# A decoder block on one core: the mixing of the cross-attention as a band with far sums, and work moved between VectorE, ScalarE and GpSimd

## What is computed

```python
emb = norm(x) + ctx
q, k, v = emb @ wq + bq, emb @ wk + bk, emb @ wv + bv
w   = pos_bias * (abs(t - j) < 64)              # 512 x 512, zero outside a band
ek  = exp(k - max over tokens of k)
ew  = exp(w - max over j of w)                  # shared by the batches
num = einsum('tj,bjd->btd', ew, ek * v)
den = einsum('tj,bjd->btd', ew, ek)
attn = (sigmoid(q) * num / den) @ wo + bo
a   = layernorm(attn + emb) * gamma + beta
out = layernorm(relu(a @ w1 + b1) @ w2 + b2 + a) * gamma + beta
```

## Time and profile before

| | us |
|---|---|
| median of 3 runs | 1067.69 (1066.9 to 1068.81) |
| the profiled execution | 1065.92 |
| its span | 1064.2 |

### The profile page before, as it was taken

The page is one execution under the profiler, slowest core; times in us unless marked ns, Lnnn a source line. Parts: engine busy times, 40 slices in busy tenths (PEclk is TensorE's granted clock), DMA queues, the critical chain, the costliest instruction groups (busy, mean ns, idle before and its releaser), DMA issues.

```text
span 1064.2 us, 18107 instructions
## 1 busy us (share of the span) xinstructions
PE 986.2 (93%) x5720; PEld 778.7 (73%) x5720; DVE 702.2 (66%) x1823; ACT 558.1 (52%) x1218; POOL 390.3 (37%) x408
## 2 busy tenths in 40 slices
PE   5889979999999979999999799998999999889987
PEld 3667765677676857777777588886777777668876
DVE  7668976366575677677778555565777777735553
ACT  4556741404030327777777644444777777754432
POOL 5211613113130366666666300115565656510030
PEclk9889989999999999999999899999999999989989
DMA  9000102000000000000001020000000000000010
GB/s 335 12 1 0 64 16 104 1 1 0 0 0 1 1 21 1 2 21 0 21 0 33 23 77 8 0 21 1 2 22 0 21 0 25 16 11 10 0 55 25
DMA packets 14332, 25.36 MB, mean 24 GB/s; under 512 B 848, under 2 KB 11208, under 8 KB 13512
## 3 DMA queue, kind: packets, MB, share of 16 engines
q1 hardware_dynamic: 14280, 24.72, 6.8%
HBM read 20.53 MB, written 2.10 MB: 21 GB/s over the span
## 4 chain that ended last, share of the span: by engine, by line
PE 70%; DVE 16%; issue 7%; ACT 4%; POOL 2%; DMA 0%; POOLq 0%; DVEq 0%; ACTq 0%
PE bank L1478 28%; PE bank L1670 5%; PE bank L1764 5%; PE bank L1622 5%; PE bank L1883 5%; PE bank L1791 4%; PE bank L1810 4%; PE bank L1776 4%; DVE conv L627 3%; PE bank L1743 2%; PE bank L1802 2%; PE bank L1633 1%; PE bank L1750 1%; DVE scores L933 1%; DVE hidden L1078 1%
## 5 line engine op out<-in xcount | busy, mean ns | idle before, releaser
L1339 ACT ACTIVATE probs<-scores,row_bias,q_rnorm 128x256 f32<-128x256 f32 (+1 forms) x256 | 143.7, 565 | 10.8 <-DVE row_bias L939 10.3
L933 DVE CUSTOM_DVE_ANT_0 scores<-bank,mask 128x256 f32<-128x256 f32 (+1 forms) x256 | 89.3, 385 | 21.5 <-PE bank L1764 17.6
L491 POOL TENSOR_TENSOR norms<-norms,minus_half 128x16 f32<-128x16 f32 x32 | 93.6, 2924 | 2.7
L1478 PE MATMUL bank<-wqkv_hi,x_hi 128*128 128x512 f32 x192 | 85.6, 446 | 2.6 <-DVE rot L907 1.4
L474 POOL TENSOR_TENSOR k_tok<-rot 128x512 f32<-128x512 f32 x32 | 41.2, 1287 | 100.7 <-DVE rot L907 100.7
L1478 PE MATMUL bank<-wqkv_hi,x_lo 128*128 128x512 f32 x192 | 77.2, 402 | 0.0
L1478 PE MATMUL bank<-wqkv_lo,x_hi 128*128 128x512 f32 x192 | 77.2, 402 | 0.0
L1764 PE MATMUL bank<-k_t,q_t 64*128 64x256 f32 (+1 forms) x512 | 67.3, 382 | 10.3 <-DVE row_max L933 8.8
L1078 DVE SCALAR_TENSOR_TENSOR hidden<-bank,lcols,hidden 128x512 f32<-128x512 f32 (+1 forms) x48 | 35.9, 749 | 60.2 <-PE bank L1478 52.5
L1776 PE MATMUL bank<-ident,probs 128*128 128x128 f32 x448 | 67.5, 280 | 5.2 <-ACT probs L1339 5.0
L1311 ACT ACTIVATE squares<-bank 128x512 f32<-128x512 f32 x64 | 38.3, 598 | 60.9 <-PE bank L1478 60.9
(11 more groups left out here) (236 smaller groups left out, 2624.0 us busy)
## 6 DMA issues: line engine op xcount, KB each, us to landing
w_stage<-in_wm_l_dram SPq DMA_DIRECT2D x8, 534.0 KB, 3.6
w_stage<-in_wqkv_dram SPq DMA_DIRECT2D x2, 1536.0 KB, 7.6
out_dram<-stream SPq DMA_DIRECT2D x4, 512.0 KB, 2.9
stream<-in_x_dram SPq DMA_DIRECT2D x1, 1536.0 KB, 12.9
emb<-in_ctx_dram SPq DMA_DIRECT2D x1, 1536.0 KB, 6.7
inner<-in_w_gate_dram SPq DMA_DIRECT2D x1, 1152.0 KB, 8.9
ew<-in_pos_bias_dram SPq DMA_DIRECT2D x1, 1024.0 KB, 9.8
w<-in_w_x_dram SPq DMA_DIRECT2D x1, 1024.0 KB, 12.8
```

The lines of the kernel that those rows point to most:

```text
L491: pool.tensor_tensor(norms[:, 2, :], norms[:, 1, :], minus_half[:, :], ALU.pow).then_inc(c_rn, 1)
L933: dve.tensor_tensor_reduce(scores[:, i % 2, e, 0:nk], bank[6 + e][:, (i % 2) * 2 * P:(i % 2) * 2 * P + nk], mask[:, 2 * P - nk:2 * P], 1.0 ...
L1339: act.activation(probs[:, i % 2, e, 0:nk], scores[:, i % 2, e, 0:nk], ACT.Exp, bias=row_bias[:, w % 2, h:h + 1], scale=q_rnorm[:, w, h:h + 1],
L1478: ins = pe.matmul(out, stationary, moving, start=(first and i == 0), stop=(last and i == len(terms) - 1))
```

## The change

- `mix_tokens`: each group of four products of 512 columns becomes four of 192, 320, 320 and 192 columns (`NEAR`), which cover the key tiles within reach of each range of tokens: 1024 columns instead of 2048.
- The rest comes as far sums. ACT sums each 128-column tile of ek and ekv over its tokens (`tile_sum`: a Copy with an accumulator, 16 for each block): those of block 0 in a row after `by_token(0)`, those of block b+1 in pairs after each of the eight Relu of `mlp_x(b)`. POOL adds two tile sums for each of three ranges (`far_keys`: three additions of 128x4), once all 16 of the block are there. DVE adds ew_t times the far sum to den and to num (`with_far`: three instructions of 192, 128 and 192 columns each), so that `gated_ratio` has 18 instructions instead of 6, and waits for `b_far` first.
- DVE's `embed` of block 2 stands ahead of `gated_ratio(1)`, and that of block 3 at the end of round 0, after `a_low(1)`.
- The four `tensor_scalar` of `norm_apply` into `inner` go from DVE to POOL (`norm_inner`), for all four blocks; DVE keeps the statistics.
- POOL's order: `far_keys(0)` stands between `keep_emb(0)` and `rstd_of(5)`; `far_keys(b+2)` stands in `finish(b)` ahead of the remaining `rstd_of`, `keep_emb` and `add_out(b)`.
- DVE's and POOL's loops over blocks are written out; PE's and ACT's stay loops.

```diff
+NEAR = ((0, 0, 192), (2, 192, 512), (1, 0, 320), (3, 320, 512))
+FAR = ((2, 3), (0, 3), (0, 1))
+FAR_RANGES = ((3, 0, 192), (3, 192, 320), (0, 320, 512))
...
+            def far_keys(b):
+
+                pool.wait_ge(b_sums, 16 * b + 16)
+                if b:
+                    pool.wait_ge(b_ratio, 8 * b)
+                for r, (j0, j1) in enumerate(FAR):
+                    pool.tensor_tensor(far_sums[:, :, r], tile_sums[:, :, j0], tile_sums[:, :, j1], ALU.add)\
+                        .then_inc(b_far, 1)
...
             keep_emb(0)
+            far_keys(0)
             rstd_of(NB + 1)
             keep_emb(1)
...
+            def norm_inner(b):
+
+                rstd_of(2 * NB + b)
+                pool.wait_ge(n_rstd, 2 * NB + b + 1)
+                for t in range(TT):
+                    ins = pool.tensor_scalar(inner[:, b * TT + t, :], stream[:, b * TT + t, :], mean_var[:, t, 0:1],
+                                             rstd[:, t:t + 1], ALU.subtract, ALU.mult)
+                ins.then_inc(b_res, 1)
+
+            def finish(b):
+
+                rstd_affine(2 * b + 1, 1 if b < NB - 2 else 0)
+                rstd_affine(2 * b + 2, 0 if b < NB - 2 else 1)
+                if b + 2 < NB:
+                    far_keys(b + 2)
+                if b + 3 < NB:
+                    rstd_of(NB + b + 3)
+                    keep_emb(b + 3)
                 add_out(b)
-                if nxt:
-                    add_b2(b + 1)
-                rstd_of(2 * b + NB + 3 if norm2 else b + 2 * NB)
+                add_b2(b + 1)
+                norm_inner(b)
+
+            rstd_of(NB + 2)
+            keep_emb(2)
+            far_keys(1)
+            for b in range(NB - 1):
+                finish(b)
...
             add_out(NB - 1)
             rotate(1, 1)
-            rstd_of(3 * NB - 1)
+            norm_inner(NB - 1)
             rnorm(1, 1)
...
+            def with_far(out, near, s):
+
+                for r, (j, t0, t1) in enumerate(FAR_RANGES):
+                    ins = dve.scalar_tensor_tensor(out[:, t0:t1], ew_t[:, j, t0:t1], far_sums[:, s, r:r + 1],
+                                                   near[:, t0:t1], ALU.mult, ALU.add)
+                return ins
...
+                dve.wait_ge(e_tp_out, TT)
+                dve.wait_ge(b_far, 3 * b + 3)
                 for m in range(KD):
...
+                    with_far(y[:, m, :], den, m).then_inc(b_ratio, 1)
+                    dve.wait_ge(b_ratio, 8 * b + 4 * m + 1)
+                    dve.scalar_tensor_tensor(y[:, m, :], eq[:, m, :], 1.0, y[:, m, :], ALU.add, ALU.mult)\
+                        .then_inc(b_ratio, 1)
+                    dve.wait_ge(b_ratio, 8 * b + 4 * m + 2)
+                    dve.reciprocal(y[:, m, :], y[:, m, :]).then_inc(b_ratio, 1)
                     dve.wait_ge(b_aft, 4 * b + 2 * m + 2)
-                    dve.tensor_tensor(y[:, m, :], y[:, m, :], num[:, :], ALU.mult).then_inc(b_y, 1)
+                    with_far(full_num, num, KD + m).then_inc(b_ratio, 1)
+                    dve.wait_ge(b_ratio, 8 * b + 4 * m + 4)
+                    dve.tensor_tensor(y[:, m, :], y[:, m, :], full_num[:, :], ALU.mult).then_inc(b_y, 1)
...
             a_low(0)
+            embed(2, NB + 2)
             dve.wait_ge(wx_lo, 7)
             gated_ratio(1)
 
-            def mixing(b, norm2):
-                if norm2:
-                    embed(b + 2, 2 * b + NB + 2)
+            def mixing(b):
+                if b < NB - 2:
...
                     a_low(b + 1)
+                    if b + 3 < NB:
+                        if b:
+                            dve.wait_ge(b_res, b)
+                        embed(b + 3, NB + b + 3)
...
                 dve.wait_ge(b_x2, b + 1)
-                norm(2 * b + NB + 3 if norm2 else b + 2 * NB, b, to_inner=True)
-                if norm2:
+                norm_stats(2 * NB + b, b)
+                if b < NB - 2:
                     gated_ratio(b + 2)
...
+            def tile_sum(b, i):
...
+                act.activation(sum_scratch[:, i % 2, :], ek_ekv[:, sm // KD, sm % KD, j * P:(j + 1) * P], ACT.Copy,
+                               accum_out=tile_sums[:, sm, j:j + 1]).then_inc(b_sums, 1)
...
+                    if nxt:
+                        tile_sum(b + 1, 2 * c)
+                        tile_sum(b + 1, 2 * c + 1)
...
             by_token(0)
+            for i in range(4 * TT):
+                tile_sum(0, i)
             transposed_emb(1)
...
-                        for j in range(TT):
-                            ins = pe.matmul(bank[2 + (2 * m + i + 2) % 4][:, :], src[:, j, m * P:(m + 1) * P],
-                                            ew_t[:, j, :], start=(j == 0), stop=(j == TT - 1))
+                        for n, (j, t0, t1) in enumerate(NEAR):
+                            ins = pe.matmul(bank[2 + (2 * m + i + 2) % 4][:, t0:t1], src[:, j, m * P:(m + 1) * P],
+                                            ew_t[:, j, t0:t1], start=(n == 0), stop=(n == len(NEAR) - 1))
```

## The result

The changed kernel took 1084.9 us (median of 4 runs, 1081.07 to 1088.71) against 1067.3 of the kernel before: a ratio of 1.017, 95% interval 1.0152 to 1.0188. It is slower, as forecast, but by 17.6 us where 4.4 were forecast, and outside the range of 1062 to 1081. The profiled execution took 1085.3 us with a span of 1083.6, against 1064.2 before: +19.4.

The account below looks back on a forecast made before the run. PE was taken as the bound in cross-attention. Halved mixing products against waits for y, clock losses, +0.9 behind the loop and -0.5 at the handover summed to +4.4 us: 1070.3 profiled, 1072.1 median; 8-in-10 range 1062 to 1081.

Parts of the forecast that it names:

- The bound and the products: PE bounds the cross-attention; its mixing products fall from 14.00 to 7.0 us a block, saving 28 us over four.
- Tile sums: ACT's sums take 0.31 us per instruction pair, bounds 0.25 and 0.48, delaying mixing 0.6 us in blocks 1 to 3.
- rival B: Sums on ACT take 0.48 us each and pace that engine: +12.8 us, 1080.5; chance 0.16.
- The ratio: DVE's ratio with its far terms takes 13.6 us for both chunks of a block, bounds 12.8 and 15.0.
- Block 0: y ready at 189.6 instead of 180.84 us, +8.8, plus 1.8 for PE's slowed clock: +10.6 when the block ends.
- Block 1: +0.6 us for the sums, -7.0 from the products, nothing waits: running total +4.2 at its first MLP product.
- Block 2: +0.6 and -7.0 us, with 4.0 lost again to y 2.9 late and 1.1 of DVE backlog: running total +1.8.
- rival D: VectorE and GpSimd contend: norm_inner stretches the ratio's two gate steps by half in three blocks, +2.1 us, 1074.2; chance 0.08.
- Block 3: PE waits 6.7 us for y; the projection starts +2.2 late, plus 1.8 for the clock: running total +4.0.
- Behind the loop: norm_inner(2) puts four tensor_scalar on POOL ahead of the first x tile, 0.55 us each, 2.2 together; taken as +0.9.
- The handover: DVE is spared 2.00 us waiting for rstd and 1.38 more, but POOL's rnorm(1) starts 2.1 later: -0.5, bounds -3.3 and +2.1.
- Rival A: Stalls end in block 0, so later ratios meet PE in time: -8.2 us, 1059.5; milder form 1065 to 1067; chance 0.22 together.

Follow-up runs that it names:

- shift form: Changed kernel with GpSimd's normalisation written as x * rstd + shift (mult and add, shift = -mean * rstd) instead of subtract and mult: 1078.96 us, ratio 1.0099 to before.

## Why the prediction was right in direction and wrong in size

- **The bound and the products.** Right. 7.17 us for 32 banded matmuls against the forecast 7.0.
- **Tile sums.** Right at 0.29 us a pair against 0.31 (4.64 us for 16), so rival B had no ground. The far additions took 0.50, as forecast.
- **The ratio.** 13.2 us where nothing stretches it (block 1: 222.32 to 235.53), against 13.6: the estimate of 1.0 us for three ranges was right (0.99 measured).
- **Block 0.** The mechanism, DVE behind `rstd_of(5)` behind the far sums, is the [7.87 <-POOL rstd] above. From M0 the projection started 9.7 us late, where 8.8 were forecast: the gate step's extra 1.34 and 0.4 on the product of y, less some 0.4 each for the earlier far sums and the shorter ratio. The clock cost 2.1 (from +9.7 at the projection to +11.8) instead of 1.8. Together 1.2 us worse than forecast.
- **Block 1.** The step of -6.4 is right: 11.8 to 5.4.
- **Block 2.** The queue was foreseen, its size was not: the block gives +0.4 where I had -2.4. Its projection starts 4.1 us late, where 0.7 was forecast. 1.2 of that come from block 0, 2.1 from the stretched L771 (rival D's mechanism), 0.6 from the addition L798, which stands behind y and which the trace names as what released PE; the shorter ratio gives 0.4 back. Behind the wait of 4.89 the clock falls and costs 1.8, which the sum left out because I expected too short a wait; the 1.1 of backlog that it had there did not come. Rival D was weighed at 0.08 and placed on the gate steps beside `norm_inner`. Beside `norm_inner` the gate steps and products took 0.69 to 0.86, nearly nothing; it came beside `keep_emb`, in blocks 0 and 2, and in block 2 it lengthened the very wait behind which the clock fell.
- **Block 3.** The step is right: +2.3 measured, +2.2 forecast, wait 6.36 against 6.7. In its parts it is 0.0 up to the projection and 2.3 for the clock, where I had 0.4 and 1.8.
- **Behind the loop: the step that failed.** "0.55 each" is the term that was mis-sized. The earlier trace rows gave a copy and a mult and add, and I read them as prices of a `tensor_scalar` in general. This one is a subtract and mult and costs 1.22 us, and the first of the four at this place 2.13, beside VectorE's subtractions: 5.74 us for the four instead of 2.2, of which the price makes 2.7 and the one long instruction 0.9. All of it lies between `rstd` and the first x tile, where the kernel before had nothing:

```profile
364.11 1.02 POOL L356 TENSOR_TENSOR rstd<-var_eps,minus_half 128x4 f32<-128x4 f32 x1
...
365.14 0.80 POOL L466 COPY x_tile<-inner 128x256 f32<-128x256 f32 x2
```

  In that timeline of POOL in the kernel before, the copy starts 0.01 us after the power. PE's 4.20 us of wait and the half clock behind it (2.5 us on the down product, 0.5 on the transposes) make 7.2 of the +7.5, where I had +0.9. The kernel in shift form is the check: at the price that I had assumed (0.56, and 1.3 us for the shift) the wait is 1.90 and the clock stays, and the step is +2.2 (from 205.5 to 226.0 us after M0, where the kernel before has 195.58 and 213.83).
- **The handover.** The same term again: 4.85 us of normalisation stand ahead of the power of `rnorm(1)`, and k waits for that, where I had it 2.1 later. +3.9 for -0.5, outside my bound of +2.1, which had been worked out from the same 0.55.

Two of six steps carry 11.0 of the missing 15.1 us, and both rest on one price. In the shift form they come to 2.2 and 0.9 us instead of 7.5 and 3.9, so some 8 of the 11 hang on the price; the other 3 or so these terms would have missed at 0.55 too, and where they arise stays open. Block 2 carries 2.8 and block 0 1.2. Rival A did not come: the stalls of blocks 2 and 3 were both there. Its 1059.5 is passed only by kernels that also change the order in the last round (1057.44 and 1052.92); with the far sums moved alone, block 3's wait stays at 4.8 us. The direction was right for the reason given: at block 3's MLP, ahead of both these steps, the kernel is already 8.1 us late, where 4.0 were forecast.

The Trainium skill (TensorE: Matmul & The Clock Gate, HAM oscillation) was cited for the clock falling again after each wait. The trace agrees in four places, with windows at 0.50 to 0.76, and the runs show where it does not happen: after waits of 1.31, 1.68 and 1.90 us. The Trainium skill (SBUF — State Buffer, Who interferes with whom) says that a VectorE instruction with two inputs in SBUF contends with a GpSimd instruction that reads SBUF. The runs agree: with two inputs 0.69 became 2.03. With one input there, the gate step from PSUM stayed at 0.69 and the reciprocal at 3.35.

## What to carry to other kernels

Before an operation is moved to another engine, price it by a row of the same kinds of operation on that engine, not by the same instruction name; and if there is none, widen the range well beyond the nearest rows, since here the price lay outside their spread (0.51 for a copy, 0.98 for twice the columns). A moved operation's place in its new queue matters as much: ask which waiting instruction stands ahead of what others need. An intermediate result that moves from PSUM to SBUF can expose VectorE's next step to GpSimd. When a wait of TensorE's cannot be shortened, put other work in it, useful work if there is any.

## What the runs showed of the hardware

- GpSimd's `tensor_scalar` on 128x256 fp32 took, in the median, 408 ns as mult and add with constants, 558 with two columns, 1072 as subtract and mult with constants, and 1223 with columns. VectorE took 1.38 to 1.57 us for four of the last form.
- 96 fp32 transposes against the identity, 0.111 us each, kept the granted clock at 1.00 where TensorE otherwise waits 12.9 us and the window has 0.88: in this kernel transposes count as work for the clock.
- A VectorE step with two inputs in SBUF makes little headway while a GpSimd addition of 128x1024 (2.35 us) runs beside it: a step of 0.69 us took 2.03 and 2.54 and ended 0.54 and 0.55 us after the addition, and one of 0.47 took 2.58. With one input in SBUF, the gate step that reads PSUM (0.69) and the reciprocal (3.35) are not stretched beside the same addition.
